# Output projection by the seven-product identity, on a ring of four sub-blocks

## The reference, cut to what matters

```python
c = x @ W.T + b + 2.0 * (x @ A[id]) @ B[id]           # conditioning, a LoRA per sequence
q, k, v = rope(c @ wq), rope(c @ wk), c @ wv          # 32 query heads, 8 kv heads, of 128
o = softmax(causal(q k / sqrt(128))) @ v              # per sequence of 64
x1 = x + o @ wo                                       # wo: 4096 x 1024, the output projection
out = x1 + ffn(cond2(x1))                             # folded base product, two routed LoRAs
```

## Time and profile before

| | before |
|---|---|
| device time, median of 3 | 2761.23 us |
| profiled execution, device time | 2761.87 us |
| its span, first to last instruction | 2759.7 us |
| PE busy / DVE / POOL / ACT | 2693.2 / 1595.8 / 1010.0 / 853.4 us |
| mean granted clock of TensorE | 0.992 of full |
| output projection, first half | 872.2 to 1236 us |
| output projection, second half | about 2170 to 2534 us |

### The profile page before, as it was taken

One profiled execution on the slowest core, in us unless ns is written; L12 is line 12 of the kernel. 1 busy time (PEld: TensorE's weight loads), 2 busy tenths in 40 slices (PEclk: granted clock), 3 DMA queues, 4 the chain that ended last, 5 costly groups with the idle time before them and its releaser, 6 DMA issues.

```text
span 2759.7 us, 40669 instructions
## 1 busy us (share of the span) xinstructions
PE 2693.2 (98%) x13432; PEld 2223.4 (81%) x13432; DVE 1595.8 (58%) x2355; ACT 853.4 (31%) x2039; POOL 1010.0 (37%) x678
## 2 busy tenths in 40 slices
PE   8989899999999999999998989999999999999999
PEld 7868788888887888877887878888888788887887
DVE  2124566666777666665525356666667765666452
ACT  2223344444443212121203334444444321122120
POOL 0030766666663222220303076666666222221020
PEclk9999999999999999999999999999999999999999
DMA  6872222222214323211445122222222432231332
GB/s 213 212 209 72 73 66 74 77 77 78 71 60 145 123 80 110 91 54 56 113 134 147 46 73 77 78 77 72 68 77 77 143 110 92 98 106 39 84 92 71
DMA packets 281654, 263.15 MB, mean 95 GB/s; under 512 B 67834, under 2 KB 217466, under 8 KB 281474
## 3 DMA queue, kind: packets, MB, share of 16 engines
q1 hardware_dynamic: 235106, 202.11, 24.7%
q10 hardware_dynamic: 46368, 58.73, 6.0%
HBM read 195.06 MB, written 65.73 MB: 95 GB/s over the span
## 4 chain that ended last, share of the span: by engine, by line
PE 89%; issue 3%; SPq 2%; DVE 2%; POOL 2%; DMA 1%; ACT 1%; DVEq 0%; ACTq 0%; POOLq 0%
PE prod L742 27%; PE prod L744 26%; PE prod L743 26%; PE turned L934 4%; PE turned L959 2%; PE turned L946 1%; PE turned L736 1%; POOL slot_f L1658 1%; POOL slot L1663 1%; SPq L551 1%; SPq L526 1%; PE prod L1160 0%; PE turned L924 0%; DMA raw<-in_wv 0%; PE prod L788 0%
## 5 line engine op out<-in xcount | busy, mean ns | idle before, releaser
L2088 DVE TENSOR_TENSOR x<-prod,x 128x512 f32<-128x512 f32 x512 | 347.2, 689 | 265.5 <-PE prod L744 264.9
L1706 POOL TENSOR_TENSOR w_lo<-raw,w_hi 128x1024 fp32r<-128x1024 f32 x64 | 157.0, 2454 | 578.6 <-ACT w_hi L1462 578.6
L742 PE MATMUL prod<-c_hi,w_hi 128*128 128x512 f32 (+1 forms) x832 | 328.6, 395 | 9.3 <-DVE q_rot L2003 5.9
L744 PE MATMUL prod<-c_hi,w_lo 128*128 128x512 f32 (+1 forms) x832 | 325.0, 391 | 0.0
L743 PE MATMUL prod<-c_lo,w_hi 128*128 128x512 f32 (+1 forms) x832 | 324.7, 390 | 0.0
L742 PE MATMUL prod<-c_hi,slot 128*128 128x512 f32 x768 | 309.4, 403 | 15.7 <-ACT p_sum L1382 12.6
L744 PE MATMUL prod<-c_hi,slot 128*128 128x512 f32 x768 | 301.4, 392 | 0.0
L743 PE MATMUL prod<-c_lo,slot 128*128 128x512 f32 x768 | 300.9, 392 | 0.0
L1997 DVE TENSOR_TENSOR rope_sin<-prod,consts_sb 64x512 f32<-64x512 f32 x320 | 220.3, 688 | 97.0 <-PE prod L744 84.2
L742 PE MATMUL prod<-x_hi,w_hi 128*128 128x512 f32 x656 | 261.4, 398 | 9.1 <-DVE h_masked L1846 3.8
L744 PE MATMUL prod<-x_hi,w_lo 128*128 128x512 f32 x656 | 257.2, 392 | 0.0
(11 more groups left out here) (189 smaller groups left out, 4965.9 us busy)
## 6 DMA issues: line engine op xcount, KB each, us to landing
o_scratch<-o_f ACTq DMA_DIRECT2D x64, 512.0 KB, 3.1
raw<-in_wo SPq DMA_DIRECT2D x64, 512.0 KB, 3.3
raw<-t_scratch SPq DMA_DIRECT2D x34, 512.0 KB, 3.5
raw_a<-in_wq SPq DMA_DIRECT2D x32, 512.0 KB, 5.0
raw<-in_wq SPq DMA_DIRECT2D x32, 512.0 KB, 4.8
c_lo_f<-o_scratch SPq DMA_DIRECT2D x32, 512.0 KB, 4.9
o_xf<-o_scratch SPq DMA_DIRECT2D x32, 512.0 KB, 5.3
t_scratch<-x ACTq DMA_DIRECT2D x17, 512.0 KB, 4.8
```

Source lines behind the costliest of these rows:

```text
L742: pe.matmul(dst, wh, xh, start=start, stop=False, skip_group_check=skip)
L744: return pe.matmul(dst, wl, xh, start=False, stop=stop, skip_group_check=skip)
L1706: pool.tensor_tensor(WL[j % 2][:], RAW[j % 2][:], WH[j % 2][:].bitcast(F32), ALU.subtract).then_inc(split_d, 1)
L2088: dve.tensor_tensor(X1[:, xs], PJ[q % 4][:], X1[:, xs], ALU.add).then_inc(taken, 1)
```

## The change

The output projection becomes a product by the seven-product identity. The k axis (4096) is cut into 16 sub-blocks u (`SUBS`; two heads each, of which one head stands in the first block row and one in the second), the output rows into four pairs (r, r + 4), the tokens into the two column blocks. One slot is the seven products of one row pair over up to four sub-blocks that stand in a ring of four places in SBUF. There are 19 slots: slot s drops the oldest sub-block, takes in sub-block s, and works on row pair (s + 1) mod 4. So slots 0, 1, 2 have 1, 2, 3 k-tiles, slots 3 to 15 have 4, slots 16, 17, 18 have 3, 2, 1. Matmuls per half: 16 x 4 x 7 x 3 = 1344. The new sub-block is last in each product.

The operands on the side of the tokens are the attention outputs of two heads and four sums of them: POOL makes the sums (`parts`), beside `weights` in the attention stage, and ACT writes them to DRAM (`parts_store`). Each operand is then loaded (256 KB), cast by ACT and subtracted by DVE, in sub-blocks 0 and 1 by POOL. Weights: five sums and four lo parts by POOL, three lo parts by DVE, in slot 0 all seven by POOL. X1 stands in eight separate tiles in this stage, over the freed tiles of attention, and is copied back by ACT in the last stage. The loop over groups becomes straight code of 19 slots on every engine.

```diff
+def k_tiles(s):
+    return max(0, s - SUBS + 1), min(4, s + 1)
+def row_of(s):
+    return (s + 1) % 4
@@ SP @@
+                def load_part(u, n):
+                    if u == 0:
+                        sp.wait_ge(a_prod, hf * A_STEP["a_prod"] + (NP * (PAIRS - 1) + n + 1))
+                    elif u >= 4:
+                        sp.wait_ge(b_prod, hf * (NP * SLOTS_B) + (NP * (u - 1) + n + 1))
+                    hold(sp)
+                    sp.dma_start(part(n)[2][:, u % 4], o_d[NP * u + PART[n]]).then_inc(o_in[n][u % 2], 16)
...
+                load_b_raw(0)
+                load_b_raw(1)
+                load_parts(0)
+                load_parts(1)
+                sp.wait_ge(comb, hf * A_STEP["comb"] + (NC * (PAIRS - 1) + C12 + 6))
+                hold(sp)
+                load_row(1)
+                load_row(5)
+                load_b_raw(2)
...
+                for s in range(3, SLOTS_B):
+                    if s + 2 < SLOTS_B:
+                        load_b_raw(s + 2)
+                    if s + 1 < SUBS:
+                        load_parts(s + 1)
@@ PE @@
+                TAIL = {(0, P1): [(turn_p, 5)], (0, P6): [(pv, 5), (score, 6)], (0, P7): [(score, 7)],
+                        (1, P2): [(turn_p, 6)], (1, P5): [(pv, 6)], (1, P4): [(turn_p, 7)], (2, P6): [(pv, 7)]}
...
+                    for n in OPS:
+                        for f, u in TAIL.get((s, n), ()):
+                            f(B, u)
+                        if n in RAW_LO and s >= POOL_W:
+                            pe.wait_ge(b_vlo, hf * VLO_HALF + vlo_count(s, n))
+                        else:
+                            pe.wait_ge(b_wlo, hf * WLO_HALF + wlo_count(s, n))
+                        if n == P2:
+                            pe.wait_ge(b_p1, hf * SLOTS_B + (s + 1))
+                        elif n in (P7, P3):
+                            pe.wait_ge(x1_step, xb + (X_OPS * s + {P7: X12A, P3: X22A}[n]))
+                        elif s == 0:
+                            pe.wait_ge(qk_in, hf * A_STEP["qk"]
+                                       + qk_count(PAIRS - 1, {P1: R11, P6: R22, P5: R12, P4: R21}[n]))
+                        else:
+                            pe.wait_ge(x1_step, xb + (X_OPS * (s - 1) + {P1: X11, P6: X21A, P5: X12, P4: X21}[n]))
@@ ACT @@
+                TAIL = {(0, 0): [(take_p, 5)], (0, 2): [(o_store, 5)], (0, 5): [(exp, 6)], (0, 9): [(exp, 7)],
+                        (1, 3): [(take_p, 6)], (1, 5): [(parts_store, 2)], (1, 6): [(o_store, 6)],
+                        (1, 9): [(take_p, 7)], (2, 3): [(o_store, 7)], (3, 9): [(parts_store, 3)]}
+                STEPS = [("p1", 0, 0), ("o", 0, P4), ("w", 1, P1), ("w", 1, P6), ("o", 0, P3), ("w", 1, P2),
+                         ("o", 1, P1), ("w", 1, P5), ("o", 1, P6), ("w", 1, P7), ("o", 1, P2), ("w", 1, P4),
+                         ("o", 1, P5), ("w", 1, P3), ("o", 1, P7)]
...
                 m_hi(0, "ar1")
+                for r in range(KC):
+                    act.copy(X1[:, r * TOK:(r + 1) * TOK], X1O[r][:]).then_inc(x1_cp, 1)
@@ POOL @@
+                def parts(b, stored, n_part):
+                    for w in range(2):
+                        pool.wait_ge(o_out[w], stored + (16 * b + 16 + 16))
+                    b11, b21, b12, b22 = (OF[:, i * NT:(i + 1) * NT] for i in range(4))
+                    n = n_part + 4 * b
+                    pool.tensor_tensor(b11, b12, b11, ALU.subtract).then_inc(part_in, 1)
+                    pool.tensor_tensor(b12, b22, b12, ALU.subtract).then_inc(part_in, 1)
+                    pool.wait_ge(part_in, n + 1)
+                    pool.tensor_tensor(b22, b22, b11, ALU.subtract).then_inc(part_in, 1)
+                    pool.wait_ge(part_in, n + 3)
+                    pool.tensor_tensor(b21, b22, b21, ALU.subtract).then_inc(part_in, 1)
...
                     lo(P2, a12)
+                    if lp >= 4 and (lp - 1) % 3 != Q23:
+                        parts(2 * ((lp - 3) // 3) + ((lp - 1) % 3 == Q01), B["stored"], B["part"])
                     add(SLF[P5][:, NT:2 * NT], a21, a22, ALU.add, P5)
...
+                    add(s2, a21, a11, ALU.subtract)
+                    pool.wait_ge(b_sum, hf * (5 * SLOTS_B) + (5 * s + 1))
+                    add(s2, s2, a22, ALU.add)
+                    if 1 <= s <= POOL_O:
+                        o_lo(s - 1, P3)
+                    if s < POOL_W:
+                        lo(P1, a11)
+                    lo(P6, s2)
+                    if s < POOL_W:
+                        lo(P2, a12)
+                    if s == 1:
+                        o_lo(1, P1)
+                        parts(2, B["stored"], B["part"])
+                    if s == 0:
+                        o_lo(0, P1)
+                    if s == 4:
+                        parts(3, B["stored"], B["part"])
+                    add(f32(P5), a21, a22, ALU.add, P5)
+                    lo(P5, f32(P5))
...
@@ DVE @@
-                    if last:
-                        o_lo(0, 0, hf * (4 * NKV))
...
+                    w_lo_b(s + 1, P1)
+                    o_lo(s, P4)
+                    formed(P6)
+                    dve.wait_ge(b_p1, hf * SLOTS_B + (s + 1))
+                    dve.tensor_tensor(bank[P6], P1S[:], bank[P6], ALU.add).then_inc(x1_step, 1)
+                    if s < 4:
+                        for h in range(2):
+                            dve.wait_ge(x_in[row_of(s) + 4 * h], hf * 32 + 32)
+                        hold(dve)
+                    stepped(U2B)
+                    add(x12, bank[P6])
+                    o_lo(s, P3)
+                    if s == 0:
+                        before_exp(B, 6)
+                    formed(P2)
+                    add(x11, bank[P2])
+                    if s == 1:
+                        normalise(B, 7)
+                    w_lo_b(s + 1, P2)
+                    o_lo(s + 1, P1)
+                    formed(P5)
+                    add(x22, bank[P5])
...
+                    if s >= SUBS:
+                        x_lo_of(s - 1)
```

More of the change, by code:

```diff
@@ L101 @@
 S_N = S_B + KC
-SPLIT_D = D_N + 1
+SPLIT_D = 1
 TW_W, TW_A2, TW_B = 0, KC, KC + 1
@@ L660, in _ @@
[L660 to L673, removed]
@@ L744, in three, with main @@
                 return pe.matmul(dst, wl, xh, start=False, stop=stop, skip_group_check=skip)
-            def main(q, s, t, XHi, XLo, start=True, stop=True, m=P, chunk=lambda k: None):
-                for k in range(KC):
+            def main(q, s, t, XHi, XLo, start=True, stop=True, m=P, chunk=lambda k: None, ks=tuple(range(KC))):
+                for k in ks:
                     chunk(k)
@@ L1066, in _ @@
+                for s in range(SLOTS_B):
+                    slot(s)
                 x_base = pe.snap(hf * (TT * KC))
@@ L1279, in b1_cols @@
                     act.copy(view(BCH[s][:], TT), view(B1S[:], TT)[:, :, bass.ds(j, P)]).then_inc(bc_in, 1)
-                A_NAMES = ("a_prod", "comb", "s_sum", "raw", "unit", "tb", "stored", "head")
+                A_NAMES = ("a_prod", "comb", "s_sum", "raw", "unit", "tb", "stored", "part", "row")
                 def weight_hi(B, lp, n):
@@ L1687, in weights @@
                     lo(P3, SLF[P3][:, NT:2 * NT])
-                names = ("a_prod", "s_hi", "s_sum", "raw")
+                names = ("a_prod", "s_hi", "s_sum", "raw", "stored", "part")
                 B = a_bases(pool, hf, 0, names)
-                weights(B, 0)
+                for lp in range(3):
+                    weights(B, lp)
                 with pool.Fori(0, LOOPS) as turn:
                     B = a_bases(pool, hf, turn, names)
-                    for lp in range(1, 7):
+                    for lp in range(3, 9):
@@ L1709, in _ @@
+                for s in range(SLOTS_B):
+                    weights_b(s)
                 pool.wait_ge(wd_hi, hf * SPLIT_D + SPLIT_D)
@@ new lines, in o_lo, with x_lo_of @@
+                def o_lo(u, n):
+                    if not POOL_O <= u < SUBS:
+                        return
+                    hi, lo, f = part(n)
+                    dve.wait_ge(b_ohi, hf * (NP * SUBS) + (NP * u + n + 1))
+                    dve.tensor_tensor(lo[:, u % 4], f[:, u % 4], hi[:, u % 4].bitcast(F32), ALU.subtract
+                                      ).then_inc(b_olo_v, 1)
+                def x_lo_of(s):
+                    for i in range(4 * (s - SUBS + 1), 4 * (s - SUBS + 2)):
+                        r, t = X_ORDER[i]
+                        xs = slice(r * TOK + t * NT, r * TOK + (t + 1) * NT)
+                        hi_is(H_X1 + i)
+                        dve.tensor_tensor(CL[:, xs], X1O[r][:, t * NT:(t + 1) * NT], CH[:].bitcast(F32)[:, xs],
+                                          ALU.subtract).then_inc(x1_lo, 1)
@@ L2114, in _ @@
+                for s in range(SLOTS_B):
+                    slot(s)
+                x_lo_of(SLOTS_B - 1)
                 hi_is(H3["a2"])
```

503 lines of the change are left out of this document (292 added, 211 removed).

## The result

| | before | after |
|---|---|---|
| device time, median | 2761.99 us | 2739.09 us (2737.32 to 2743.29, 4 runs) |
| ratio | | 0.9916, 95% interval 0.9898 to 0.9933 |
| profiled span | 2759.7 | 2737.8 |
| matmuls | 13432 | 13048 |

A forecast was written before the change was run, and what follows sets the result against it. PE, busy 98% of the span, bounds the kernel. Per half 366.8 becomes 304.5 + 8.4 + 24 + 2.9 = 339.8, gain 27.0; twice 54, less 3, gives 51: 2761.9 to 2711 us, range 2682 to 2748.

The forecast's parts named there:

- 1, matmuls: Output projection: 192 fewer matmuls per half, 384 in all, at 0.2266 us each, 87.0 us saved on the path.
- 2, full slots: Slots 3 to 15: 19.03 us each, DVE busy 16.6 us and POOL 12, all hidden; cost 0.
- rival C: DVE, blocked by POOL, bounds full slots at 23.2 us: 2820 us; chance 0.07, shared with anything else slower.
- 3, sums in attention: Attention stage: POOL's sums of attention outputs delay its queue; 3 us for the whole run, bounds 0 and 16.
- rival B: Small waits, 1 us in each of 26 full slots, plus some of attention's 13 us: 2740 us; chance 0.23.
- 4, the seam: First slots after attention: POOL's serial work and queue order lose 24 us a half, bounds 5 and 40.
- T: End of the last attention pair, from which times in slots 0 and 1 are counted; forecast at 870.7.
- The clock's 2 us on top: Slot 1: short products between gaps run partly at slow clock, mostly hidden in waits; 2 us more.
- the sign named for this step: Sign of being right: 20 to 28 us of PE gaps in slots 0 and 1, ended by POOL, ACT and DVE.
- 5, after slot 18: End of slot 18 and start of `small`: 2.9 us of waits in place of 1.69, bounds 1.5 and 8.
- 6, X1 copies: Last stage: ACT copies X1 back in 8.4 us, hidden ahead of the next exp; cost 0, up to 2.

The follow-up runs named there:

- e8: Changed kernel with the attention-output sums of only the last two sub-blocks (slots 1 and 4) cut to 16 of 512 columns: 2719.41 us.
- e2: Changed kernel with DVE doing before_exp(6) ahead of X12A in slot 0: 2723.37 us, ratio 0.9862 to the kernel before.
- e9: Changed kernel with ACT issuing the store of parts(2) in slot 0, ahead of exp(7), not in slot 1: 2735.23 us.
- e3: Changed kernel with the four subtractions of parts(3) spread one each over slots 4 to 7, store in slot 7: 2730.56 us.
- e11: Changed kernel with rows 1 and 5 first, exp(6) first, last sums spread, lo parts of sub-block 1 by DVE, and early store: 2699.56 us.
- e4: Changed kernel with the lo parts of sub-block 1 made by DVE in place of POOL: 2719.27 us, ratio 0.9848 to the kernel before.

## Why the prediction was right and wrong, by its own steps

**1, matmuls: right.** 384 fewer; 11 slots of 84 in 209.44 us are 0.2267 each (the view counts one more, which began before the stretch).

**2, full slots: right.** 19.04 us, no gap; DVE 171.38 / 11 = 15.6 busy per slot against 16.6 forecast, POOL 13.2 against 12. DVE's subtractions took from 0.68 to 1.78. So rival C did not come, though single instructions were as slow as it feared. The lock of the Trainium skill (SBUF — State Buffer, SBUF: two separate sides) is seen in the single rows, 1.78 for 0.68 here and POOL's 1.74 for 1.29 under e8 (the two rows 954.07 and 954.58 overlap), and not in the length of a full slot.

```profile
954.58 1.78 DVE L2294 TENSOR_TENSOR c_lo<-c_lo_f,c_hi 128x512 fp32r<-128x512 f32 x1
```

**3, sums in attention: right in kind,** 3 us forecast, 0 to 2 measured. The upper bound of 16 was summed wrongly: the sums stand in 14 pairs of each half, so 1 us in each would be 28, and rival B's 13 would be 25. In the stretch that answers to the earlier trace rows, POOL went from 12.63 to 14.29 busy in 18 us without a gap of PE:

```profile
689.00:707.00 18.00, 18.00 (x91) 15.15 (x91) 11.36 (x17) 3.10 (x6) 14.29 (x12) 1.00 0.16 59
```

**4, the seam: this step failed by size,** 24 us a half forecast, 32.1 measured (12.3 + 19.3 + 0.6 in slots 0, 1, 2). The mechanism was the one named: POOL's serial work, ACT's queue, o_lo(2, P1). POOL's work was sized nearly right as a whole: from its first subtraction of sub-block 1 at 891.92 to the last sum of slot 2 at 913.7, 21.8 us for 22.7, though it holds six of the seven subtractions counted, and 2.0 us of waits for ACT where 1.1 were counted. P3 of slot 1 was put at T + 42.4 and started at T + 50.0; two terms make that up.
- Its start. I put it at T + 15.7; it was T + 19.2, 3.5 us later. I had rows 1 and 5 landing so that X12A came at T + 10.2, where the trace has T + 13.3: SP issued them behind all parts at T + 4.8, and they shared 353 GB/s with them. e2 took the wait for the rows out of this path altogether, and the stage lost 6.3 and 6.8 us in the two halves.
- The landing of a store. From POOL's last sum to P3 of slot 1 I had 4.0 us (38.4 to 42.4); the trace has 9.0 (T + 41.0 to T + 50.0). The 5.1 us between the issue of parts_store(2) and its landing, for which o_store(6) waits, were not in the sum. e9 took 3.4 and 3.0 us off the stage; new gaps of 1.05 and 1.17 us in slot 2 gave part of the 5.1 back.

The clock's 2 us on top were right, behind this path: P3 took 2.73 us for 1.36, and slot 2 15.98 for 15.4. Before it, the slow clock fills time in which PE would have waited. So the sign named for this step, 20 to 28 us of gaps in slots 0 and 1, came true at 21.6, while these two slots lost 31.5: gaps alone do not measure a seam. (Slot 2's matmuls are 14.3 us, not the 13.6 of the prediction; nothing rests on it.)

**2 again, slot 4: the second step that failed.** "Cost 0" for the full slots took parts(3) for granted. The working of step 2 counted 9 POOL instructions per slot, 12 us; slot 4 has 13, at 1.74 for three of them. With the 13.2 us that nine took in a full slot that is 19.7, more than the slot of 19.04, before any wait of POOL for a cast. Measured 5.3 us a half: e3 put the four sums into four slots and the 5.3 were gone.

**5, after slot 18:** 3.3 for 2.9 (8.10 us for 4.76 of matmuls). **6, X1 copies: right.** They stand where they were put, and the exp behind them runs 21.9 after the first product of `small` (1248.10 - 1226.16), 21.5 before:

```profile
1239.06 7.68 ACT L1688 COPY x<-x_row 128x1024 f32<-128x1024 f32 x8
1248.10 0.21 ACT L1691 ACTIVATE route_s<-route_s 128x8 f32<-128x8 f32 x1 [1.36 <-DVE route_s L2451]
```

The sum: 8.1 in the seam, 5.3 in slot 4, 0.4 at the end, 14 a half and 28 in all, which is what is missing (51 - 23). From T to the first product of `small` the trace has 353.5 us in the first half and 353.4 in the second, 13.7 over the forecast's 339.8 in each. Rival B has the time almost to the microsecond, 2740, and is still wrong: it had small waits in every slot, and slots 5 to 15 have none. That e11 comes to 2699.6, below the forecast, says that the forecast's seam was not a floor: what it took as a serial chain of POOL could be put into idle time or given to DVE. Open: what the seam would gain at full clock. The trace gives 10.5 us of longer matmuls in slots 0 to 2, but by the path of step 4 PE would have waited instead for most of it, and no run could set the clock apart from the gaps that it follows.

## What to carry to other kernels

In a seam, add up the lost time of each slot and not only the gaps of PE. Follow each in-order queue to the instruction that begins the longest serial piece of work behind it: a wait of DVE for a row cost more through ACT's exp and POOL's start than at PE. Count the landing of a store as a term wherever its tile is written again, and issue the store where its data is ready. A budget of busy time per slot says nothing of the one slot with four instructions more; check that one by itself, and put such extra work where its engine stands idle in its own queue.

## What the runs showed of the hardware

The clock. After the gap of 6.88 us, the 16 score matmuls took 3.68 us (e4, above); after one of 0.41 they took 2.00 (e2). In slots 0 and 1 the granted clock was 0.70 and 0.78 of full, so that part of each stretch ran at the lower level of 1.2 GHz, and it was 1.00 in slots 5 to 15. Behind the gap of 7.12 us all of a stretch ran at the lower level, and behind one of 2.40 us in slot 4 part of one did (changed kernel):

```profile
887.00:891.00 4.00, 3.63 (x17) 3.64 (x18) 1.78 (x4) 2.73 (x17) 0.00 (x0) 0.50 1.05 387
969.50:975.00 5.50, 5.50 (x17) 4.38 (x18) 5.47 (x5) 2.50 (x5) 4.62 (x4) 0.69 0.86 243
```

In e11 slots 0 to 2 still have 0.87, and the stretch after them has 1.00:

```profile
873.64:926.56 52.92, 44.42 (x219) 34.17 (x218) 45.83 (x65) 30.32 (x83) 38.48 (x34) 0.87 0.87 293
926.56:951.00 24.44, 24.43 (x108) 19.92 (x107) 22.15 (x24) 12.28 (x24) 19.93 (x13) 1.00 0.41 123
```

The transfers. In slot 0 of the changed kernel all 16 DMA engines were busy throughout (a share of 1.01 at 353 GB/s). From 872.69 to 894.20 us a part of 256 KB took 6.2 us from issue to landing, longer than 512 KB took in the kernel before (4.9 over the whole run):

```profile
c_lo_f<-o_scratch SPq DMA_DIRECT2D x9, 256.0 KB, 6.2
```
